# Three context products side by side in a pipelined attention slot, with six transposed-probability tiles

## What is computed

```python
q = heads(x @ Wq + bq)                  # 6 heads of 64
k = heads(x @ Wk + bk)
v = heads(x @ Wv + bv)
scores = q @ k.T / 8                    # 256 x 256 for each head
probs = softmax(where(adj, scores, scores - 9e15))
ctx = probs @ v                         # 256 x 64 for each head
x = layernorm(x + ctx @ Wf + bf)
```

## Time and profile before

| quantity | value |
|---|---|
| time, median of three runs | 2974.87 us |
| the profiled execution's own time | 2970.94 us |
| its span, first to last instruction | 2969.1 us |
| PE busy | 2917.2 us, 98% |
| PE weight loads busy | 2642.2 us, 89% |
| DVE busy | 2558.7 us, 86% |
| ACT busy | 2417.7 us, 81% |
| POOL busy | 1270.0 us, 43% |
| mean granted TensorE clock | 0.999 |

### The profile page before, as it was taken

How to read it: one execution, slowest core, us unless ns; L and a number is a source line. 1 busy time by engine, 2 the same in 40 slices (tenths; PEclk the granted TensorE clock), 3 DMA queues, 4 the chain that set the end, 5 groups by cost and what they waited for, 6 DMA issues and landing times. The chain is left out here.

```text
span 2969.1 us, 72423 instructions
## 1 busy us (share of the span) xinstructions
PE 2917.2 (98%) x22432; PEld 2642.2 (89%) x22432; DVE 2558.7 (86%) x8649; ACT 2417.7 (81%) x6888; POOL 1270.0 (43%) x1262
## 2 busy tenths in 40 slices
PE   8999999999999999999999999999999999999997
PEld 7888888888889999999999999999999999999996
DVE  6999999999888888888888888888888888888887
ACT  7999999999987777777777777777777777777775
POOL 3777777666642333422322333423323223233233
PEclk9999999999999999999999999999999999999999
DMA  2111111110123222222233222322222222323221
GB/s 91 36 36 36 36 36 36 36 36 31 35 77 103 76 78 72 77 76 75 74 80 103 78 76 72 83 71 75 79 73 75 78 74 74 80 71 82 72 76 50
DMA packets 153211, 198.76 MB, mean 67 GB/s; under 512 B 48896, under 2 KB 115328, under 8 KB 152448
## 3 DMA queue, kind: packets, MB, share of 16 engines
q1 hardware_dynamic: 152832, 194.13, 23.8%
HBM read 68.24 MB, written 50.33 MB: 40 GB/s over the span
## 5 line engine op out<-in xcount | busy, mean ns | idle before, releaser
L500 POOL TENSOR_TENSOR residual<-x,br 128x384 f32<-128x384 f32 x192 | 188.9, 1007 | 1345.3 <-DVE mix L1031 1331.9
L726 ACT ACTIVATE probs<-logits,nmax 128x256 f32<-128x256 f32 x1152 | 573.9, 503 | 52.5 <-DVE nmax L1001 52.5
L78 PE MATMUL pj<-xt_hi,w_lo 128*128 128x256 f32 x1728 | 493.6, 286 | 0.0
L79 PE MATMUL pj<-xt_lo,w_hi 128*128 128x256 f32 x1728 | 482.8, 279 | 0.0
L80 PE MATMUL pj<-xt_hi,w_hi 128*128 128x256 f32 x1728 | 482.6, 279 | 0.0
L1001 DVE CUSTOM_DVE_ANT_0 logits<-s,mask 128x256 f32<-128x256 f32 x1152 | 433.1, 420 | 6.0
L597 ACT ACTIVATE g_exps<-g_v,g_nmax 128x256 f32<-128x256 f32 x768 | 384.9, 514 | 2.5 <-DVE g_nmax L907 0.4
L1022 DVE TENSOR_SCALAR probs<-probs,recs 128x256 f32<-128x256 f32 x1152 | 363.9, 358 | 20.5
L719 ACT ACTIVATE stack<-split 64x512 fp32r<-64x512 f32 x576 | 360.8, 626 | 5.7
L78 PEld LDWEIGHTS pj<-xt_hi,w_lo 128*128 128x128 f32 x1728 | 324.2, 188 | 36.9 <-issue 36.6
L711 ACT ACTIVATE split<-pj,bc 128x256 fp32r<-128x256 f32 x576 | 242.0, 471 | 133.7 <-PE pj L80 130.8
(11 more groups left out here) (122 smaller groups left out, 8340.8 us busy)
## 6 DMA issues: line engine op xcount, KB each, us to landing
stack<-split SPq DMA_DIRECT2D x576, 128.0 KB, 2.3
y<-out SPq DMA_DIRECT2D x128, 384.0 KB, 2.7
x<-y SPq DMA_DIRECT2D x96, 384.0 KB, 3.1
x<-x SPq DMA_DIRECT2D x32, 384.0 KB, 3.1
adj<-adj SPq DMA_DIRECT2D x128, 64.0 KB, 3.1
w_whole<-att_w SPq DMA_DIRECT2D x3, 2304.0 KB, 12.4
g_w_stage<-gat_w SPq DMA_DIRECT2D x2, 576.0 KB, 6.2
br<-att_b_row SPq DMA_DIRECT2D x3, 192.0 KB, 5.9
```

Source lines behind the costliest of these rows:

```text
L78: pe.matmul(out, a[1], b[0], start=first, stop=False)
L79: pe.matmul(out, a[0], b[1], start=False, stop=False)
L726: last = act.activation(probs[:, (HEADS * u + h) % 4, t, :], logits[:, h % 2, t, :], ACT.Exp, scale=-1.0, bias=nmax[:, u, h, t:t + 1], acc ...
```

## The change

The PE's order in a slot becomes T2, X, S0 (of `cur`), C0, C1, C2, Q0, S1, V0, T0, Q1, S2, V1, Q2, B0, T1, B1. The three context blocks stand together, S0 comes in the slot of its own sample, and T0 and B0 come earlier. C2 no longer goes to the context banks in turn, but to `pj_ps[0]`, which it has between x0 and v0; the order of the two `pj` banks no longer changes with the sample. V0 waits until DVE has written the remainder of C2 (`ct_split`), and C2 waits for the remainder of x0. There are six tiles of transposed probabilities instead of four. The lists of ACT and DVE are put in another order to match. The scores of the second sample leave `crossing`. No arithmetic is added or left out.

```diff
-    g_PT_BUFS, PT_BUFS = 2 * g_QUAD, 4
+    g_PT_BUFS, PT_BUFS = 2 * g_QUAD, 6
...
-        cx_two = [cx_ps, pj_ps[2]]
+        cx_banks = [cx_ps, pj_ps[2], pj_ps[0]]
...
-        BANK_ORDER = ("x0", "x1", "qk0", "v0", "qk1", "v1", "qk2", "back0", "back1")
+        BANK_ORDER = ("x0", "x1", "ctx2", "qk0", "v0", "qk1", "v1", "qk2", "back0", "back1")
...
-            return pj_ps[(u + BANK_ORDER.index(what)) % 2]
+            return pj_ps[BANK_ORDER.index(what) % 2]
...
-            def make_v(half, u, t, layer):
+            def make_v(half, u, t, layer, prev=None):
+                if t == 0 and prev:
+                    pe.wait_ge(ct_split, at(DC, *prev, DC))
...
-            def pair_of_contexts(half, u, c):
+            def pair_of_contexts(half, u, c, nxt):
+                if c < 2:
+                    pe.wait_ge(ct_split, at(DC, half, u, c + 1 - DC))
+                elif nxt:
+                    pe.wait_ge(pj_read, split_of(*nxt, X[0]))
+                else:
+                    pe.wait_ge(back_read, at(NT, half, u, 1 - NT))
...
-                pe.wait_ge(ct_split, at(DC, half, u, c - 1))
```

More of the change, by code:

```diff
@@ L731, in even_pt @@
                 act.wait_ge(transposed, at(HEADS, half, u, 2 * c + 1))
-                act.wait_ge(contexts, at(DC, half, u, c - 1))
+                act.wait_ge(contexts, at(DC, half, u, c + 1 - DC))
                 act.activation(pt_sb[:, pt_slot(u, 2 * c)], pt_ps[0][:, :, :], ACT.Identity).then_inc(pt_even_read, 1)
@@ L737, in high_ct @@
                 act.wait_ge(back_made, at(NT, half, u, -NT))
-                act.activation(ct_hi[u][:, c, :], cx_two[(DC * u + c) % 2][:, 0:N], ACT.Identity, bias=bc[:, layer, V, c:c + 1]).then_inc(ct_hi_done, 1)
+                act.activation(ct_hi[u][:, c, :], cx_banks[c][:, 0:N], ACT.Identity, bias=bc[:, layer, V, c:c + 1]).then_inc(ct_hi_done, 1)
             def slot(cur, nxt, prev, layers, opening=False, part=None):
@@ L751, in slot @@
                     even_pt(*prev, 1)
+                if cur:
+                    own_rows(*cur, 2)
                 if nxt:
@@ L754, in slot @@
                     high_xt(*nxt, 1)
-                if cur:
-                    own_rows(*cur, 2)
                 if prev:
+                    even_pt(*prev, 2)
                     high_ct(*prev, 0, prev_layer)
@@ L763, in slot @@
                 if prev:
-                    even_pt(*prev, 2)
-                if nxt:
-                    high_qk(*nxt, 0, nxt_layer)
+                    high_ct(*prev, 2, prev_layer)
                 if cur:
@@ L769, in slot @@
                 if nxt:
+                    high_qk(*nxt, 0, nxt_layer)
                     own_rows(*nxt, 0)
-                if prev:
-                    high_ct(*prev, 2, prev_layer)
                 if cur:
@@ L776, in slot @@
                 if nxt:
+                    copy_v(*nxt, 0)
                     high_qk(*nxt, 1, nxt_layer)
-                    copy_v(*nxt, 0)
                 if cur:
+                    exp(*cur, 3)
                     even_pt(*cur, 0)
-                    exp(*cur, 3)
                 if nxt:
@@ L1007, in odd_pt @@
                 dve.wait_ge(transposed, at(HEADS, half, u, 2 * c + 2))
-                dve.wait_ge(contexts, at(DC, half, u, c - 1))
+                dve.wait_ge(contexts, at(DC, half, u, c + 1 - DC))
                 dve.tensor_copy(pt_sb[:, pt_slot(u, 2 * c + 1)], pt_ps[1][:, :, :]).then_inc(pt_odd_read, 1)
@@ L1012, in low_ct @@
                 dve.wait_ge(ct_hi_done, at(DC, half, u, c + 1))
-                dve.scalar_tensor_tensor(ct_lo[u][:, c, :], cx_two[(DC * u + c) % 2][:, 0:N], bc[:, layer, V, c:c + 1], f32(ct_hi[u][:, c, :]),
+                dve.scalar_tensor_tensor(ct_lo[u][:, c, :], cx_banks[c][:, 0:N], bc[:, layer, V, c:c + 1], f32(ct_hi[u][:, c, :]),
                                          ALU.add, ALU.subtract).then_inc(ct_split, 1)
@@ L1044, in slot @@
                     low_xt(*nxt, 0)
+                if prev:
+                    odd_pt(*prev, 2)
+                if nxt:
                     low_xt(*nxt, 1)
@@ L1047, in slot @@
                     mask_and_max(*cur, 0)
+                if prev:
+                    low_ct(*prev, 0, prev_layer)
+                if cur:
                     mask_and_max(*cur, 1)
+                    normalise(*cur, 0)
                 if prev:
-                    odd_pt(*prev, 2)
-                    low_ct(*prev, 0, prev_layer)
+                    low_ct(*prev, 1, prev_layer)
+                    low_ct(*prev, 2, prev_layer)
+                if cur:
+                    normalise(*cur, 1)
                 if nxt:
@@ L1055, in slot @@
                 if cur:
-                    normalise(*cur, 0)
                     mask_and_max(*cur, 2)
-                    normalise(*cur, 1)
                     mask_and_max(*cur, 3)
-                if prev:
-                    low_ct(*prev, 1, prev_layer)
+                    normalise(*cur, 2)
                 if cur:
-                    normalise(*cur, 2)
+                    odd_pt(*cur, 0)
                 if nxt:
@@ L1067, in slot @@
                 if cur:
-                    odd_pt(*cur, 0)
                     mask_and_max(*cur, 4)
-                if prev:
-                    low_ct(*prev, 2, prev_layer)
-                if cur:
                     normalise(*cur, 3)
@@ L1078, in slot @@
                     low_qk(*nxt, 2, nxt_layer)
-                if prev:
-                    add_back(*prev, 0)
                 if cur:
@@ L1084, in slot @@
                 if prev:
+                    add_back(*prev, 0)
                     add_back(*prev, 1)
@@ L1419, in pair_of_contexts @@
                         h = 2 * c + s
-                        last = pe.matmul(cx_two[(DC * u + c) % 2][rows_of(s), 0:N], v_sb[u][:, kt, h * HEAD_DIM:(h + 1) * HEAD_DIM], pt_sb[:, pt_slot(u, h), kt, :],
+                        last = pe.matmul(cx_banks[c][rows_of(s), 0:N], v_sb[u][:, kt, h * HEAD_DIM:(h + 1) * HEAD_DIM], pt_sb[:, pt_slot(u, h), kt, :],
                                          start=kt == 0, stop=kt == NT - 1)
@@ L1430, in slot @@
                     transpose_x(*nxt, 1, opening)
+                if cur:
+                    pair_of_scores(*cur, 0)
                 if prev:
-                    pair_of_contexts(*prev, 0)
-                    pair_of_contexts(*prev, 1)
+                    pair_of_contexts(*prev, 0, nxt)
+                    pair_of_contexts(*prev, 1, nxt)
+                    pair_of_contexts(*prev, 2, nxt)
                 if nxt:
@@ L1438, in slot @@
                     pair_of_scores(*cur, 1)
-                if prev:
-                    pair_of_contexts(*prev, 2)
                 if nxt:
-                    make_v(*nxt, 0, nxt_layer)
+                    make_v(*nxt, 0, nxt_layer, prev)
+                if cur:
+                    pair_of_transposes(*cur, 0)
+                if nxt:
                     make_qk(*nxt, 1, nxt_layer)
@@ L1446, in slot @@
                     pair_of_scores(*cur, 2)
-                    pair_of_transposes(*cur, 0)
                 if nxt:
@@ L1450, in slot @@
                     make_qk(*nxt, 2, nxt_layer)
+                if prev:
+                    make_back(*prev, 0, nxt, prev_layer)
                 if cur:
                     pair_of_transposes(*cur, 1)
[L1454 to L1457, removed]
                 if prev:
@@ L1514, in crossing @@
                 pair_of_transposes(*first, 1)
-                pair_of_scores(*second, 0)
             pe.wait_ge(g_ident_loaded, 16)
```

## The result

| | before | after |
|---|---|---|
| time, median of the runs | 2974.86 us (2969.27 to 2975.39) | 2952.68 us (2952.33 to 2955.01) |
| ratio | | 0.9933 [0.9922, 0.9945] |
| the profiled execution's own time | 2970.94 us | 2952.37 us |
| its span | 2969.1 us | 2950.5 us |

The forecast was 2957 us, in 2940 to 2972. The kernel takes 4.3 us less than that. Profiled execution against profiled execution, the scale in which the forecast was worked out, the change saves 18.6 us where 14.4 were expected. Between the medians it saves 22.2 us: the one trace of the kernel before is of an execution 3.9 us under its median, and nothing here shows what its slower executions spent.

A forecast was written before the change was run, and what follows sets the result against it. PE was taken to bound the kernel: a slot falls from 22.07 us, or 22.16 with weight splitting, to 21.70 + 0.24 = 21.94, saving 14.4 us from 2970.94, hence 2957 us, range 2940 to 2972.

The forecast's parts named there:

- PE sets the pace, and blocks are priced by their distance and neighbours: PE, busy 700.00 of 700 us; each block priced from its start to the next block's start, depending on its neighbours.
- price of X to S: PE, S0 directly after X: entry taken as 0.08 us, as B after T shows.
- Natural slot 21.70: PE's new slot with nothing waiting: block lengths sum to 21.70 us, 0.37 less than 22.07.
- Q1 after T: PE, projection Q1 following T0: 2.12 + 0.08 = 2.20 us.
- The two bank waits, 0.09 and 0.14: PE, Q2 late by 0.09 us and B1 by 0.14 or 0.17, awaiting evictions of Q1 and Q2; together 0.24.
- The new waits are covered: V0, C2, T0, S1, Q1 and T2 get their inputs in time; V0's load has 0.7 us of cover.
- rival 3: One more cover gives way, T2's or the chains late by twice as much: 0.1 to 0.2 us a slot, 2965 to 2974; chance 0.13.
- Rival 1: DVE's `norm0` locked out by POOL's layer-norm output, V0 late by 0.6 us, slot 22.54, kernel 3013 us; chance 0.07.
- The weight slots lose their extra: The 24 slots where POOL splits weights: their extra 0.09 us goes, from 22.16 to 21.94.
- The crossing and the last two slots unchanged, 2 us to either side: Crossing and two last slots, where DVE and ACT set the pace: left unchanged, with 2 us to either side.
- The sum: Whole kernel: 9.1 us from 70 slots plus 5.3 from 24, 14.4 us off 2970.94, giving 2957.
- What would show it: Signs in the profile: slots of 21.9 us, and PE wait rows of about 0.1 to 0.2 before Q2 and B1.

The follow-up runs named there:

- the version without the waits: Changed kernel with Q2 of every sample but the first two in the contexts' bank, B1 then waiting for Q1's remainders: 2930.02 us.
- the swap in POOL's list: Changed kernel with POOL's residual additions moved behind the layer norm's outputs: 3008.96 us in one run.
- the same, S0 in the crossing: Changed kernel with Q2 in the contexts' bank, and scores of heads 0 and 1 of the second sample back in the crossing: 2929.4 us.
- Q2 waiting: Changed kernel with Q2 in the contexts' bank, but Q2 still waiting for the remainders of Q1: 2940.79 us in one run.
- C2 apart: Changed kernel with C2 back behind S1 in the first context bank, ACT's and DVE's lists adapted: 2993.06 us, ratio 1.0062 to before.
- four tiles: Changed kernel with four tiles of transposed probabilities instead of six and the old waits on contexts: 2999.01 us in one run.
- T0 later: Changed kernel with T0 behind S2, and DVE's copy of the odd tile behind the remainders of Q1: 2976.56 us in one run.

## Why the prediction was right, point by point

- **PE sets the pace, and blocks are priced by their distance and neighbours.** Right. 14 of the 15 natural lengths came out within 0.03 (Q2 and T1 in the version without the waits), although six of the pairs of neighbours are new. The assumed price of X to S, 0.08, was right: S0's first matmul is 0.20 from the next, 0.08 more than the pace of 0.12 behind it.
- **Natural slot 21.70.** Mis-sized by 0.04: it measured 21.66 in the version without the waits (21.67 in its slots with the paces of the changed kernel). The term that failed is Q1 after T, "2.12 + 0.08 = 2.20". The entry cost 0.08 as said (1591.27 to 1591.47, 0.20), but the 17 matmuls after it ran at 1.93 / 17 = 0.1135 us each, where Q0 and Q2 run at 0.118. That is 94 x 0.07 = 6.6 us less than forecast, of which B1 (0.03 longer) and small parts give some back; what is left is 94 x 0.04 = 3.8 of the 4.3. The pace is not explained (below), so to which side the forecast missed was chance: with Q1 at its other pace, an estimate from the 0.08 that the two paces differ by, the slot would be 21.97, above the forecast's 21.94.
- **The two bank waits, 0.09 and 0.14.** Right in place and size: 0.08 and 0.14 in the slot shown, 0.24 together by the run that takes them away. They rest on the eviction chain of 2.44 us and the 0.06 from DVE to the load, and on ACT and DVE being free to start it in time: after Q1 the chain again took 2.44 (1593.40 to 1595.84), after Q2 2.45.
- **The new waits are covered.** Right. V0, C2, T0 and T2 are not late in the slot shown. `low_ct2` ends at 1588.22 and V0's load goes out at 1588.79: 0.57 of cover, 0.7 was forecast. The difference is about the 0.15 that `norm0` lost to POOL. So rival 3 did not come either.
- **Rival 1.** It did not come true: `norm0` lost 0.15, against the 0.7 from which it decides. The prediction's own row of 0.82 (0.2 more) pointed there. Its mechanism exists all the same: the swap in POOL's list brings it about.
- **The weight slots lose their extra.** Right: 21.92 in the slot shown.
- **The crossing and the last two slots unchanged, 2 us to either side.** Both moved, the first slot behind the crossing by 1.3 up and the end by 1.25 down, and cancel, which is luck. The longer half clock was not in the forecast.
- **The sum.** With 21.90 instead of 21.94 the same sum gives 94 x 0.04 = 3.8 us less, 2952.7 against 2952.4 measured. It starts from one execution of the kernel before that was 3.9 us faster than the median; counted from the median it would have said 2960.5, inside the range and 7.8 too high.
- **What would show it.** The forecast said that the list of waits would have rows for Q2 and B1. It has none; only the distances between starts show them.

## What to carry to other kernels

Where matmuls of different width or kind alternate on a busy TensorE, price each change of kind from distances between starts, put blocks of a kind side by side, and count the buffers that this takes: here the grouping was worth 0.35 us a slot, and without two more tiles it would have been lost. When a reordering brings two blocks that share a bank closer than the eviction of that bank takes, the gain is partly handed back; look for a bank that is idle at that time, since one other choice of bank here gave 22 us, as much as the whole change. Waits of 0.1 us on the TensorE, behind matmuls whose rows overlap, showed in no list of waits here: compare a block's length with that of the same block elsewhere.

## What was not expected of the hardware

**Two paces of one block.** A projection of q and k runs uniformly at one of two paces, 0.1133 or 0.1178 us a matmul, at a clock of 1.00 in both; it is worth 0.08 us a block. Counted over the 92 slots from 2 to 93:

| kernel | Q0 fast | Q1 fast | Q2 fast |
|---|---|---|---|
| before | 0 | 0 | 0 |
| changed | 0 | 92 | 0 |
| Q2 in its own bank | 33 | 67 | 0 |
| the same, S0 in the crossing | 34 | 73 | 0 |
| Q2 waiting | 3 | 45 | 0 |
| C2 apart | 0 | 0 | 0 |
| four tiles | 40 | 0 | 0 |
| POOL's list swapped | 1 | 30 | 6 |
| T0 later | 0 | 3 | 0 |

In Q1 it is most of what the expectations for Q2 waiting and for C2 apart missed, and a part with four tiles (1586.28 to 1588.28 above is 2.00 / 17 = 0.1176). No run was made that tells what decides it. It stays open, and times of such kernels that differ by less than 94 x 0.08 = 7.5 us are compared only with the paces beside them.

**How a POOL instruction holds a multiplication of DVE depends on which it is.** A free multiplication takes 0.35 us. In the changed kernel, from the second slot on, all 93 multiplications that began beside the mask (0.62 us) and all 24 beside the cast of a weight (0.51) ended 0.14 to 0.15 us after that instruction; in the swapped version all 100 that began beside a residual (1.02) ended 0.15 to 0.16 after it. So these were held to its end, and what they lost is what it still had to run: 0.19 us beside the mask in the slot shown before, and 0.75 beside the residual (1.10 instead of 0.35). The layer norm's output (1.65) holds differently. In the changed kernel a multiplication begun 0.3 us after it takes 0.50, and one begun 0.7 after it takes 0.34, not held at all, and both end long before it does. In the swapped version 88 multiplications were begun 1.07 us or more after the start of an output, and these again ended 0.14 to 0.15 after it. Why the first part of an output lets a multiplication pass is not known.
